# A decoder layer on one core: the hand-written order of its units on TensorE, ScalarE, VectorE and GpSimd is rearranged

## The reference, cut to what matters

```python
x = x + attn(layernorm(x))    # causal conv of 4 taps, SiLU; q, kg, v, g = xc @ w; gated linear attention, 8 heads
#   gk = log_sigmoid(kg) / 16; k = 1 - exp(gk); S = S * exp(gk) + k v'; o = q S; o += sigmoid(aug_w * v)
#   o = headwise norm of o; out = (silu(g) * o) @ wout
x = x + xattn(layernorm(x), ctx)   # 16 heads of 8: softmax(q k' / sqrt(8)) v, then @ Wo
x = x + ffn(layernorm(x))     # router score per token; of the 64 tokens of a sequence the 48 best get gelu(x @ w)
```

## Time and profile before

| Engine | busy us | share of the span |
|---|---|---|
| TensorE (matmul) | 274.6 | 83% |
| ScalarE | 245.9 | 74% |
| VectorE | 240.0 | 73% |
| POOL | 163.7 | 50% |

### The profile page before, as it was taken

One profiled execution on the slowest core, in us unless ns is written; L12 is line 12 of the kernel. 1 busy time (PEld: TensorE's weight loads), 2 busy tenths in 40 slices (PEclk: granted clock), 3 DMA queues, 4 the chain that ended last, 5 costly groups with the idle time before them and its releaser, 6 DMA issues.

```text
span 330.5 us, 10717 instructions
## 1 busy us (share of the span) xinstructions
PE 274.6 (83%) x4184; PEld 195.9 (59%) x4184; DVE 240.0 (73%) x588; ACT 245.9 (74%) x438; POOL 163.7 (50%) x226
## 2 busy tenths in 40 slices
PE   1697868879998899888999899889987997898861
PEld 1576636655677566655776478556854684465540
DVE  1577788689578968896789677976697657656554
ACT  6399868976988698769976997699769875862611
POOL 5145366834755445574657375728551625023630
PEclk9998999999999999999999999999999999999996
DMA  3830200020003000300020001300110010001010
GB/s 73 234 99 18 67 0 6 13 69 2 4 13 86 2 3 12 96 10 1 11 73 4 0 10 33 93 1 9 33 45 2 5 43 16 2 0 34 2 32 17
DMA packets 15730, 10.52 MB, mean 32 GB/s; under 512 B 2816, under 2 KB 13952, under 8 KB 15680
## 3 DMA queue, kind: packets, MB, share of 16 engines
q1 hardware_dynamic: 15680, 9.84, 11.2%
HBM read 4.79 MB, written 2.10 MB: 21 GB/s over the span
## 4 chain that ended last, share of the span: by engine, by line
PE 34%; issue 13%; DVE 13%; ACT 12%; POOL 7%; POOLq 0%; ACTq 0%; DVEq 0%
PE S L824 6%; PE PT L861 6%; PE PB L882 6%; ACT pr L1259 3%; PE PA L766 3%; ACT prT L1266 3%; ACT L1183 2%; PE S L839 2%; DVE nmax L1627 2%; DVE at L1573 2%; PE PT L646 2%; PE PA L782 2%; POOL rs L399 2%; POOL yout L523 2%; DVE st L1476 1%
## 5 line engine op out<-in xcount | busy, mean ns | idle before, releaser
L1627 DVE TENSOR_REDUCE nmax<-S 128x16 bf16<-128x1024 f32 x31 | 37.9, 1221 | 29.0 <-PE S L824 29.0
L1266 ACT COPY prT<-PT 128x512 f32<-128x512 f32 x62 | 36.1, 582 | 15.8 <-PE PT L861 14.8
L861 PEld LDWEIGHTS PT<-ident,pr 128*128 128x128 f32 x248 | 26.4, 140 | 29.0 <-issue 17.8
L861 PE MATMUL PT<-ident,pr 128*128 128x128 f32 x248 | 39.9, 283 | 4.2 <-ACT prT L1266 2.3
L1147 ACT ACTIVATE k_bd<-S,k_rows 128x512 f32<-128x512 f32 (+1 forms) x72 | 41.9, 645 | 0.4 <-PE S L671 0.2
L824 PE MATMUL S<-k_bd,qT 64*64 64x512 f32 x248 | 33.7, 613 | 5.5 <-ACT pr L1259 2.6
L882 PE MATMUL PB<-v_x,prT 128*64 128x18 f32 x992 | 37.3, 213 | 0.5 <-ACT prT L1266 0.2
L882 PEld LDWEIGHTS PB<-v_x,prT 128*64 128x64 f32 x992 | 32.8, 137 | 8.1 <-issue 6.8
L1259 ACT ACTIVATE pr<-S,rs 128x1024 f32<-128x1024 f32 x31 | 34.5, 1114 | 3.4 <-PE S L839 2.7
L486 POOL TENSOR_TENSOR kc<-ke,e_r 128x512 f32<-128x512 f32 x32 | 34.9, 1109 | 3.7 <-issue 3.7
L766 PEld LDWEIGHTS PA<-v_bd,at 128*64 128x64 f32 x512 | 16.6, 137 | 19.4 <-DVE at L1573 13.9
(11 more groups left out here) (171 smaller groups left out, 669.1 us busy)
## 6 DMA issues: line engine op xcount, KB each, us to landing
cT<-in_ctxT SPq DMA_DIRECT2D x7, 256.0 KB, 3.6
v_bd<-vt SPq DMA_DIRECT2D x28, 64.0 KB, 2.1
out<-yout SPq DMA_DIRECT2D x7, 256.0 KB, 3.8
q_bd<-qs SPq DMA_DIRECT2D x96, 8.0 KB
cT<-in_ctxT SPq DMA_DIRECT2D x2, 128.0 KB, 2.6
x_all<-in_x SPq DMA_DIRECT2D x1, 256.0 KB, 2.9
v_bd<-vt SPq DMA_DIRECT2D x8, 32.0 KB, 2.1
out<-yout SPq DMA_DIRECT2D x2, 128.0 KB, 3.3
```

The source lines that it names most:

```text
L861: last = nc.tensor.transpose(dst[:, P * p:P * p + P], pr_v[:, i % 2, P * (hp * n + p):P * (hp * n + p) + P], ident[:, :])
L1266: nc.scalar.copy(prT[:, 512 * n:512 * n + 512], pt_buf(g, n)[:, :]).then_inc(s_prT, 1)
L1627: nc.vector.tensor_reduce(nmax[:, XH * (i % 2):XH * (i % 2) + XH], cut(s_buf(g, i), XH, L), AX.X, ALU.max, negate=True).then_inc(s_max, 1)
```

## The change

The same calls are made, each with the same arguments; only their order within an engine's list differs, and the point at which a list is cut into opening, step and ending. The SP list is reordered too. No unit's body changes. The diff, cut to the units that matter below:

```diff
 # SP
-                load_ctx(2)
                 values_to_blocks(0)
                 values_to_blocks(1)
+                load_ctx(2)
+                queries_to_blocks(2)
                 load_ctx(3)
...
                 queries_to_blocks(3)
+                store(0)
                 values_to_blocks(3)
-                store(0)
...
 # POOL, step(n); its a is the step's b on the other engines
+                if has(a):
+                    group_norm(a)
+                route2(n)
                 if has(a + 1):
+                    spans(a + 1)
+                    clipped_spans(a + 1)
                     scaled_keys(a + 1)
...
+                scale_b2(a)
                 center_b3(b)
-                if has(n + 5):
-                    scale_a(n + 5)
                 scale_b3(b)
                 norm_b3(b)
-                scale_b2(a)
                 route(b)
...
 # TensorE, first(): up to the scores of group 0
                 transpose_x(0)
                 keep_awake(0, 1)
+                keep_awake(0, 8)
                 context_keys(0)
-                keep_awake(0, 8)
+                project_qk(0)
+                project_g(0)
+                transpose_x(1)
                 keep_awake(0, 9)
-                project_qk(0)
                 context_values(0)
-                transpose_x(1)
                 keep_awake(0, 3)
+                project_v(0)
+                aug_weights(0)
+                project_qk(1)
+                context_keys(1)
+                scores(0, 0)
...
 # TensorE, step(n)
                 project_qk(a)
+                attend(b, 1, 0)
+                attend(b, 1, 1)
+                project_g(a)
                 router(c)
                 x_scores(n, 1)
                 x_attend(n, 0, 0)
+                ffn(c)
+                x_attend(n, 0, 1)
                 less_max(n, 1)
                 project_v(a)
-                x_attend(n, 0, 1)
-                project_g(a)
-                ffn(c)
                 x_scores(n, 2)
...
                 x_values(n, 3, 1)
+                gla_out(b)
+                x_out(n)
                 context_values(a)
-                x_out(n)
-                gla_out(b)
                 x_out2(n)
                 queries(b)
                 scores(a, 0)
                 queries2(b)
-                attend(a, 0, 0)
                 scores(a, 1)
                 x_scores(b, 0)
+                attend(a, 0, 0)
                 attend(a, 0, 1)
-                attend(a, 1, 0)
-                attend(a, 1, 1)
                 transpose_x2(n)
                 less_max(b, 0)
 # TensorE, the ending
                 less_max(8, 1)
                 router(7)
                 ffn(7)
-                keep_awake(8, 23)
-                keep_awake(8, 22)
                 x_attend(8, 0, 0)
                 x_attend(8, 0, 1)
+                x_attend(8, 1, 0)
+                x_attend(8, 1, 1)
                 x_values(8, 0, 0)
 # ScalarE, step(n) and the ending
+                b_out(c)
+                a_gate(b)
+                a_values(b)
+                b_queries(n)
                 a_keys(b, 1)
...
+                b_exp(8, 0)
                 b_ffn(7)
-                b_exp(8, 0)
 # VectorE, first(): the start of group 0's gates
                 first_norm(1)
+                a_stats(2)
+                constants(0)
                 a_log(0)
...
 # VectorE, step(n)
+                a_mask(b, 0)
+                if has(a):
+                    a_conv(a, 2)
                 a_conv(a, 3)
                 a_mask(b, 1)
                 b_max(n, 0)
                 a_silu(a)
                 a_outputs(b)
                 a_sums(b)
                 a_center(b)
-                a_gate(b)
                 b_route(c)
+                a_squares(b)
                 b_max(n, 1)
+                a_log(a)
                 b_own(c)
-                a_squares(b)
-                a_log(a)
                 b_ranks(c)
                 a_scan(a)
+                a_gate(b)
                 a_spans(a)
                 b_max(n, 2)
+                b_gelu(c)
+                b_weigh(n, 0)
                 a_scaled_q(a)
...
+                b_weigh(n, 3)
                 b_result(c, 1)
-                b_weigh(n, 3)
                 a_aug(a)
                 a_residual(b)
+                if has(a + 1):
+                    a_conv(a + 1, 1)
+                b_stats2(b)
                 b_residual(n)
-                if has(a + 1):
-                    a_conv(a + 1, 2)
                 b_stats3(n)
-                a_mask(a, 0)
-                b_stats2(b)
```

More of the change, by code:

```diff
@@ L943, in first @@
+                scores(0, 0)
                 keep_awake(0, 2)
-                project_g(0)
                 keep_awake(0, 0)
-                aug_weights(0)
-                project_v(0)
-                keep_awake(0, 5)
-                keep_awake(0, 4)
-                context_keys(1)
-                keep_awake(0, 6)
-                project_qk(1)
-                scores(0, 0)
                 attend(0, 0, 0)
                 attend(0, 0, 1)
+                keep_awake(0, 5)
+                project_v(1)
@@ L956, in first @@
+                keep_awake(0, 4)
+                keep_awake(0, 6)
+                project_g(1)
                 keep_awake(0, 7)
+                context_values(1)
+                aug_weights(1)
                 input_means(0)
-                project_v(1)
-                project_g(1)
-                context_values(1)
                 transpose_o(0)
-                keep_awake(0, 11)
                 transpose_x(2)
                 gla_out(0)
+                keep_awake(0, 11)
+                queries(0)
@@ L965, in first @@
                 keep_awake(0, 13)
-                queries(0)
                 keep_awake(0, 10)
                 keep_awake(0, 12)
+                scores(1, 0)
                 queries2(0)
+                project_qk(2)
                 x_scores(0, 0)
+                scores(1, 1)
+                attend(1, 0, 0)
+                attend(1, 0, 1)
                 less_max(0, 0)
-                project_qk(2)
-                aug_weights(1)
+                attend(1, 1, 0)
+                attend(1, 1, 1)
@@ L974, in first @@
                 x_scores(0, 1)
                 x_attend(0, 0, 0)
-                scores(1, 0)
+                project_g(2)
                 x_attend(0, 0, 1)
+                less_max(0, 1)
+                project_v(2)
+                aug_weights(2)
                 x_values(0, 0, 0)
-                scores(1, 1)
-                less_max(0, 1)
-                attend(1, 0, 0)
-                attend(1, 0, 1)
-                attend(1, 1, 0)
-                attend(1, 1, 1)
+                context_values(2)
@@ L985, in first @@
+                x_values(0, 0, 1)
                 x_attend(0, 1, 0)
-                project_v(2)
-                x_values(0, 0, 1)
+                context_keys(2)
                 x_attend(0, 1, 1)
+                transpose_o(1)
                 x_values(0, 1, 0)
                 x_values(0, 1, 1)
-                context_values(2)
-                aug_weights(2)
-                context_keys(2)
+                transpose_x(3)
                 x_out(0)
-                project_g(2)
-                transpose_o(1)
+                gla_out(1)
@@ L1095, in last @@
                 x_out(7)
+                gla_out(8)
                 x_out2(7)
                 queries(8)
+                attend(8, 1, 1)
+                queries2(8)
                 keep_awake(8, 21)
-                queries2(8)
+                keep_awake(8, 23)
+                attend(8, 1, 0)
                 x_scores(8, 0)
```

346 lines of the change are left out of this document (164 added, 182 removed).

## The result

The changed kernel took 340.48 us (median of 4 runs, 338.77 to 341.31); the kernel before, run beside it on the same chip, 334.30 us. The ratio is 1.0197 with a 95% interval of 1.0151 to 1.0242: slower beyond doubt, though at the 2% border. The profiled execution of after is the fastest of its four: 338.77 us for a span of 337.04, against 332.23 and 330.5 before.

The account below looks back on a forecast made before the run. Steps were taken as close to TensorE's own work, their second half becoming VectorE's, with opening and ending as chains. Terms -1.3 (steps), +0.2 (opening), -1.0 (ending) gave -2.1 us: 335.04 to 333 us, range 324 to 341.

Parts of the forecast that it names:

- The step: Repeated step: halves of 21.65 and 12.3 us, 33.95 against 34.17; six steps -1.3 us, from -5 to +8.5.
- rival of the step: Two: waits regained, step 1.6 us less, 325 us (chance 0.27); VectorE's string bounds, step 35.6, 343 us (0.13).
- The opening: Stretch before the first step: +0.2 us taken, from -2 to +5.
- `a_log(0)` would wait for the load: Opening, VectorE: a_stats(2) stands until the large load of x lands; a_log(0) at about 20.4, 2.5 us late.
- Some 0.9 us of that comes back: Opening: ScalarE's 1.28 us table load runs during VectorE's wait, so scores(0,0) comes at about 28.3, from 26.69.
- I put `qs` of group 2 1.2 us later: Opening: group 2's qs, ahead of scores(2,0), delayed 1.2 us by the new order.
- The tail: Opening's end, from scores(2,0) to the first step: 8.9 us before, less 1.08 and 0.65, so 7.2.
- The clock's term: Opening: half clock after TensorE's stop slows project_qk(1), context_keys(1), scores(0,0); 0 to 3 us, 0.7 taken.
- the two additional table loads: Opening, ScalarE: ten table loads instead of eight, 2.56 us, of which 0 to 2.56 on the path.
- My third rival: Opening loses 5 us: load of x, slow clock and two table loads all on the path; 338 us, chance 0.12.
- the rival with the slow steps: VectorE's string becomes the bound in the step's second half; step 35.6 us, total 343 us, chance 0.13.
- The ending: After the sixth step: b_exp(8,0) ahead of b_ffn(7) and other moves take 1.0 us off, from 0 to 2.

Follow-up runs that it names:

- the second experiment of the opening: The changed kernel with constants(0) alone put ahead of a_stats(2) on VectorE; 340.39 us, ratio 1.0237.
- With the wait taken out: The changed kernel with a_stats(2) on VectorE and scale_a(2) on POOL put back where they stood before; 334.68 us, ratio 1.0056.
- the last experiment: The kernel before with one swap on ScalarE, b_exp(8,0) ahead of b_ffn(7); 334.29 us, ratio 1.0061.
- the ending's head: Changed kernel with a_stats(2) put back, plus the old order at the ending's start on TensorE and of a_values(8) on ScalarE; 334.17 us.
- The experiment on the table load: Changed kernel, a_stats(2) put back, old order at the ending's start and last stretch, of a_deviation(8) and b_exp(7,2), and of an x_attend and x_scores(7,2); 334.19 us.
- the two moves in the kernel before: The kernel before with only a_stats(2) moved ahead of a_log(0) on VectorE and scale_a(2) ahead of spans(0) on POOL; 337.61 us, ratio 1.0169.

## Why the prediction was wrong

**The step** was right in both halves (21.74 and 12.33 us measured). What it is worth was slightly off: the five steps are 0.49 us longer in all, where I had 1.0 us shorter, in part because I took 34.17 us, the third step's own time, as the measure and the five average 34.08; and in the changed kernel the first step took 34.88 us, where the next four average 34.0. The sixth, where I had 0.2 less too, took 0.70 more and is counted with the ending below. Neither rival of the step came.

**The opening** failed, as a size: +0.2 us in the forecast, +3.55 in the trace. That `a_log(0)` would wait for the load was right (20.4 forecast, 21.00 measured), and so was TensorE's stop. The failed step is the sentence "Some 0.9 us of that comes back, since ScalarE's table load of 1.28 us is done meanwhile", and with it the term that the sum took from there, "I put `qs` of group 2 1.2 us later": it came 6.22 us later. I had followed VectorE's queue past the wait but not the other engines' waits on it: `a_gates(0)` on ScalarE and `scale_a(2)` on POOL were stopped too, and the second experiment of the opening shows that the load, moved into the wait, brings nothing while POOL stands. `scores(0,0)` came at 30.63, not 28.3. With the wait taken out, `qs` of group 2 comes 1.65 us later than before, so the 1.2 was near for the new order alone; the wait's delay, 4.57 us there, was left out of it. The tail, 7.2 in the forecast, took 7.53. And I counted the wait against the place of `a_log(0)` before, when the new order by itself would have brought it at 15.50: the wait eats a gain of 2.4 us on `a_log(0)` that I had not seen. On P1 it costs 4.34 us, between the profiled executions 4.07 (338.77 against 334.70) and between the medians 5.8; the profiled execution of after is 1.7 us under its median. With 3.55 for 0.2 the forecast of -2.1 us would have been +1.25.

The clock's term was sized too low for what it touched: `project_qk(1)`, `context_keys(1)` and `scores(0,0)` take 2.26 us more at the 1.2 GHz level (5.77 against 3.51 us), where I took 0.7 of a range from 0 to 3. With the wait gone and half clock at the same units P1 was still at 77.25, no later than before; what the half clock costs on the path, no run shows by itself. The same holds for the two additional table loads, which that kernel has too.

My third rival, the opening that loses 5 us and 338 us in all, was nearest to what happened. I gave it 0.12, because `scores(2,0)` waits for transfers that might hide a part; 1.30 of the 6.22 us came back there. That 340.48 us lies just inside my range, 324 to 341, is luck: I had set its upper end just short of the rival with the slow steps, and the steps were not slow.

**The ending** failed in sign: -1.0 us in the forecast, +1.80 measured. The step that failed is the first, `b_exp(8,0)` ahead of `b_ffn(7)`: put alone into the kernel before, it makes that slower. In the changed kernel `b_exp(8,0)` starts 3.14 us after `x_scores(8,0)` (4.60 in the last experiment) and `router(7)` is not held up (4.78 us after it), yet the stretch to `b_residual(8)` is only 0.33 us shorter, 14.32 against 14.65, and in other executions with the same order there it took up to 15.12. What leads to `b_residual(8)` is VectorE's string behind POOL's routing and the last `x_values` on TensorE, which end together; I had followed neither to its end. Which of them sets the time stays open. Counted from P6, sixth step and ending together lose 2.50 us: `x_scores(8,0)` is 2.25 us late (57.85 against 55.60), the stretch behind it gains the 0.33, the one from `b_residual(8)` to `last_result(8)` loses 0.89, and the end behind that gains 0.31. Of that 0.89, 0.57 is what the half clock at `router(8)` and `ffn(8)` costs in the old order (8.63 against 8.06), which leaves 0.32 for the order in this execution. Of the 2.25 us, 1.31 fell to a stretch at half clock that met `x_scores(7,2)` in this execution (TensorE's timeline of the changed kernel):

```profile
290.70 1.90 PE L822 MATMUL S<-k_bd,qT 64*64 64x512 f32 x8 [0.16 <-ACT pr L1258]
```

It is missing in the changed kernel with the old opening, where `x_scores(8,0)` stands 56.54 us after P6. Of the 0.94 us that are left against before, the ending's head may explain 0.24, which is within the spread; the rest stays open. It may be more: three other executions with the old order up to there have `x_scores(8,0)` at 54.85 to 55.17. The experiment on the table load did not find the cause.

## What to carry to other kernels

A unit that waits for a transfer stops its whole queue, and then each queue that needs something of it: before one is moved forward, list who waits for what stands behind it on every engine, and set its price against the new order without the wait, not against the old times. Where the order is wanted and the data are late, give the data a transfer of their own: here that took the opening's loss away without moving a unit. At the end of a kernel, follow every string back from its last result before counting an earlier start anywhere else as a gain.

## What the runs showed of the hardware

The first reader of the large load of x got group 2's part only with the whole: issued at about 10.5 us, the reader started at 19.53. Split in two, with group 2's part issued at 10.37, its reader started at 14.10 and waited for nothing.

In the kernels with a stop of 3.4 to 7.3 us on TensorE in the opening, half clock followed. The window from 22 to 32 us of the changed kernel:

```profile
22.00:32.00 10.00, 5.95 (x82) 3.17 (x82) 8.22 (x16) 8.70 (x20) 6.47 (x9) 0.53 0.06 16
```

In the same stretch the kernel before was granted 0.93. At the half level matmuls put in only to keep TensorE busy stand in the way: with the two moves in the kernel before, the `keep_awake` of eight at 25.36 us takes 1.91 us, against 1.06 for the same one without them. Half clock does not need such a stop, though: with `a_stats(2)` put back, where TensorE waits 0.45 us at that place, the stretch from 20 to 32 us was granted 0.70.
